# The order of three products in the attention sums: hi by hi, lo by hi, hi by lo

## The reference

```python
xn = layernorm(x)
q, k, v = xn @ wq.T + bq, xn @ wk.T + bk, xn @ wv.T + bv
attn = softmax((q @ k.T) * 256 ** -0.5)
lora = up_aux @ (lora_up @ (lora_down @ down_aux))
out = x + attn @ v + (xn @ W.T + b) + xn @ lora.T
```

## Time and profile before

| what | before |
|---|---|
| median of 3 runs | 518.73 us (518.38 to 518.86) |
| the profiled execution | 518.57 us |
| its span, first to last instruction | 516.8 us |
| granted TensorE clock, mean | 1.000 |
| PE busy | 506.3 us (98%) in 2948 products |
| PEld busy | 448.6 us (87%) in 2948 loads |
| DVE, ACT, POOL busy | 71%, 54%, 72% |

### The profile page before, as it was taken

How to read it: one execution, slowest core, us unless ns; L and a number is a source line. 1 busy time by engine, 2 the same in 40 slices (tenths; PEclk the granted TensorE clock), 3 DMA queues, 4 the chain that set the end, 5 groups by cost and what they waited for, 6 DMA issues and landing times.

```text
span 516.8 us, 8100 instructions
## 1 busy us (share of the span) xinstructions
PE 506.3 (98%) x2948; PEld 448.6 (87%) x2948; DVE 367.4 (71%) x839; ACT 276.6 (54%) x589; POOL 373.7 (72%) x221
## 2 busy tenths in 40 slices
PE   5999999999999999999999999999999999999997
PEld 4677897989989898898989989898998989899897
DVE  4789866867589584885868767696758748376594
ACT  3746667365744747267381655736474462724450
POOL 2834785986789966999669979699678976671730
PEclk9999999999999999999999999999999999999999
DMA  8020004000040003200050100501002010000001
GB/s 238 39 82 0 1 33 173 1 41 2 26 179 1 41 1 109 96 2 41 1 197 8 42 2 0 204 1 42 0 35 90 1 42 1 41 1 2 41 9 74
DMA packets 8694, 25.04 MB, mean 48 GB/s; under 512 B 1850, under 2 KB 3792, under 8 KB 7760
## 3 DMA queue, kind: packets, MB, share of 16 engines
q1 hardware_dynamic: 7328, 24.38, 13.0%
q10 hardware_dynamic: 1328, 0.16, 0.2%
HBM read 16.15 MB, written 8.39 MB: 47 GB/s over the span
## 4 chain that ended last, share of the span: by engine, by line
PE 94%; DVE 1%; ACT 1%; issue 0%; DVEq 0%
PE o_ps L1078 12%; PE o_ps L1080 12%; PE o_ps L1079 12%; PE g_ps L998 10%; PE g_ps L1000 10%; PE g_ps L999 10%; PE s_ps L998 8%; PE s_ps L999 8%; PE s_ps L1000 8%; PE o_ps L998 1%; PE o_ps L999 1%; PE o_ps L1000 1%; ACT prod L607 1%; PE s_ps L1078 0%; PE s_ps L1080 0%
## 5 line engine op out<-in xcount | busy, mean ns | idle before, releaser
L507 POOL TENSOR_TENSOR p_lo<-s,p_hi 128x1024 fp32r<-128x1024 f32 x60 | 144.3, 2439 | 40.0 <-ACT p_hi L657 40.0
L650 ACT ACTIVATE s<-s,e 128x512 f32<-128x512 f32 x128 | 84.3, 714 | 116.3 <-DVE s L848 116.3
L1078 PE MATMUL o_ps<-v_hi,p_hi 128*128 128x258 f32 x480 | 136.5, 284 | 0.0
L1080 PE MATMUL o_ps<-v_hi,p_lo 128*128 128x258 f32 x480 | 136.0, 283 | 0.0
L1079 PE MATMUL o_ps<-v_lo,p_hi 128*128 128x256 f32 x480 | 135.8, 283 | 0.0
L1079 PEld LDWEIGHTS o_ps<-v_lo,p_hi 128*128 128x128 f32 x480 | 91.5, 191 | 1.6
L1078 PEld LDWEIGHTS o_ps<-v_hi,p_hi 128*128 128x128 f32 x480 | 90.2, 188 | 1.6
L1080 PEld LDWEIGHTS o_ps<-v_hi,p_lo 128*128 128x128 f32 x480 | 91.2, 190 | 0.0
L807 DVE SCALAR_TENSOR_TENSOR tile_max<-s_ps,e,tile_max 128x512 f32<-128x512 f32 x80 | 59.9, 748 | 32.9 <-PE s_ps L1000 30.7
L998 PE MATMUL s_ps<-xt_hi,zt_hi 128*128 128x512 f32 x192 | 75.0, 390 | 0.0
L999 PE MATMUL s_ps<-xt_lo,zt_hi 128*128 128x512 f32 x192 | 74.7, 389 | 0.0
(11 more groups left out here) (157 smaller groups left out, 988.8 us busy)
## 6 DMA issues: line engine op xcount, KB each, us to landing
out<-base SPq DMA_DIRECT2D x15, 512.0 KB, 2.7
x_sb<-in_L_attn_x SPq DMA_DIRECT2D x7, 1024.0 KB, 7.8
x_t<-in_x_t SPq DMA_DIRECT2D x6, 1024.0 KB, 5.8
x_sb<-in_L_attn_x SPq DMA_DIRECT2D x4, 256.0 KB, 6.7
out<-base SPq DMA_DIRECT2D x4, 128.0 KB, 1.9
s<-in_L_attn_wk SPq DMA_DIRECT2D x1, 256.0 KB, 3.1
s<-in_L_attn_wq SPq DMA_DIRECT2D x1, 256.0 KB, 6.2
s<-in_L_attn_wv SPq DMA_DIRECT2D x1, 256.0 KB, 6.9
```

The source lines that it names most:

```text
L507: nc.gpsimd.tensor_tensor(p_pair(g, p_lo_sb, j), s_pair(j), p_pair(g, p_hi_sb, j).bitcast(f32), ALU.subtract).then_inc(p_lo_made, 1)
L650: nc.scalar.activation(s[:, n, :], s[:, n, :], ACT.Exp, bias=e[b % 2][:, n:n + 1]).then_inc(p_made, 1)
L1078: nc.tensor.matmul(o[:, 0:D + ONES], hi, v_hi[i][:, n, 0:D + ONES], start=first, stop=False)
L1080: mm = nc.tensor.matmul(o[:, 0:D + ONES], lo, v_hi[i][:, n, 0:D + ONES], start=False, stop=last)
```

## The change

In `add_pair` the second and third product change places. The product of p_hi by v_lo is now the last of a tile and carries the stop flag of the last tile; the product of p_lo by v_hi stands between. `split_products` keeps its order.

```diff
                     nc.tensor.matmul(o[:, 0:D + ONES], hi, v_hi[i][:, n, 0:D + ONES], start=first, stop=False)
-                    nc.tensor.matmul(o[:, 0:D], hi, v_lo[i][:, n, :], start=False, stop=False)
-                    mm = nc.tensor.matmul(o[:, 0:D + ONES], lo, v_hi[i][:, n, 0:D + ONES], start=False, stop=last)
+                    nc.tensor.matmul(o[:, 0:D + ONES], lo, v_hi[i][:, n, 0:D + ONES], start=False, stop=False)
+                    mm = nc.tensor.matmul(o[:, 0:D], hi, v_lo[i][:, n, :], start=False, stop=last)
                 return mm
```

## The result

The kernel after takes 515.78 us (median of 6 runs), the one before 518.73: a ratio of 0.9945 (95% interval 0.9935 to 0.9956), 2.95 us faster, 0.55% by the ratio.

What follows compares the result with a forecast made beforehand. The prediction took PE, never waiting in the sums, to bound the kernel. Its terms, 0 + 0 + 0 + 0 - 0.001 us, left the profiled 518.57 us, so it said 518.6 us, range 517.3 to 519.8.

Steps and rivals of the forecast that it cites:

- Step 1: Products of the sums: columns plus 13.3 ns each, 361.6 ns per tile in either order; change 0.
- the rule of the prediction: Product time as columns at 2.4 GHz plus 13.3 ns: 120.8 ns for 258 columns, 120.0 for 256, 2.89 us a sum.
- Step 2: Weight loads in each tile: p_hi, p_lo, p_hi instead of p_hi, p_hi, p_lo, still three loads; taken as 0.
- The bounds beside it: Limits for the order of weights: gain of 20 ns per twelve products, 2.6 us; loss of 10 ns, 1.3 us.
- The sign that was to tell repeat from partner: Changed interval between product starts: first to second means repeated load; second to third or third to next means a partner.
- Step 3: Moving operands in each tile: v_hi, v_hi, v_lo instead of v_hi, v_lo, v_hi, changing what streams beside a load; taken as 0.
- Steps 4 and 5: PE's waits, including for p_lo: 0; end of a sum, last product two columns shorter: 0.8 ns sooner, cost 0.
- the repeated load: Two p_hi loads in a row cost the longer step; 0.3 to 2.6 us faster, priced 1.3, 517.3 us; chance 0.16.
- Colliding partners: A start slips where a load meets its new moving operand; 1.3 us slower, 519.9 us; chance 0.10.
- the shared weight: Neighbouring p_hi products save the fixed step today, lost after the change; 6.8 us slower, 525.4 us; chance 0.02.

Runs made afterwards that it cites:

- h: Kernel before, its order kept, with 256 columns in every product but the first of a sum (output incomplete): 515.80 us, ratio 0.9945.
- i: Kernel after, its order kept, with 256 columns in every product but the first of a sum (output incomplete): 515.35 us, ratio 0.9932 to before.
- k: Kernel before, its order kept, with four columns of ones instead of two (260 columns in two of three products): 516.84 us, ratio 0.9966.
- d: Kernel before with tile order p_lo by v_hi, p_hi by v_hi, p_hi by v_lo: 515.69 us, ratio 0.9942.
- f: Kernel before with tile order p_lo by v_hi, p_hi by v_lo, p_hi by v_hi: 518.53 us, ratio 0.9997.
- c: Kernel before with tile order p_hi by v_lo, p_hi by v_hi, p_lo by v_hi, except each sum's first tile: 517.40 us, ratio 0.9977.
- e: Kernel before with tile order p_hi by v_lo, p_lo by v_hi, p_hi by v_hi, except each sum's first tile: 516.70 us, ratio 0.9964.

## Why the prediction was wrong, point by point

What bounds the kernel: right. PE had no waits in the sums, and what the products gave up, 2.97 us in the traces, reached the end in full (2.95 by the medians).

Step 1, columns and fixed steps: this failed, and the rest followed from it. The 13.3 ns beyond the columns were read from 512-column products and put on the short ones, and sums of 2.89 then looked like the floor. Measured, a 256-column product costs 118 ns (h, i), 11.3 beyond its columns. By that, an estimate of a sum without excess is 24 x 118 + 16 x 2 / 2.4 = 2845 ns; the sums before stood 0.04 to 0.06 us above it, the sums after, at 2.855, have next to no excess. The estimate isn't a proven floor: for k it gives 24 x 118 + 16 x 4 / 2.4 = 2859 ns, and k took 2.85 us. That the rule of the prediction gave 2.89, the length measured, was a coincidence: the step that was too large stood in for the excess.

Step 2, the order of weights at 0: right in its value, shown by d and f. The bounds beside it were the useful part: 20 ns in every twelve products, 2.6 us. That the sums gave back just these 2.6 us is partly luck, for the bound was read from one sum behind another: its twelve gave back 40 ns by rows rounded to 10 (1.46 to 1.42), the sums behind 512-column products about half of that. The sign that was to tell repeat from partner didn't work: the interval from first to second product shrank most (0.50 to 0.47), which was to mean the repeat, and d shows that it wasn't the repeat. "There is next to no excess that another order could remove" is the statement that was wrong.

Step 3, the order of moving operands at 0: this is the term of the sum that failed. It was weighed only as partner of a load, and it measured -2.6 us in the sums and -0.4 us behind them: d and the kernel after, which share only the order of moving operands, have the same 451.00 us, f and the kernel before the same 453.97. Why this order costs less stays open.

Steps 4 and 5, waits and the end of a sum: right; PE's three waits are still those of the setup.

The rivals: the repeated load named the right sign, and its upper end, 2.6 us, is what the sums gave back, but that is luck: its mechanism is refuted by d. Colliding partners and the shared weight did not come; by the repeated loads of d at full speed, nothing is lost or gained by keeping a weight beside its like.

## What to carry to other kernels

Where TensorE is never waiting, compare starts of short products with a variant of their own length, not with a rule from longer ones: here the excess to be gained stood in the unevenness of the steps (0.11 to 0.13), while the sums looked like the floor. The order of products that share an accumulation can be chosen; none of the six orders costs an instruction, and here they spread over 3 us. Take in what follows the short products, which can eat a part of the gain (c, e). Such a gain hangs on lengths and row spacing (it was gone with rows 320 words apart), so it has to be measured again when either changes.

## What the runs showed of the hardware

- More columns can be faster: 260 columns in two of three products gave sums of 2.85 us where 258 gave 2.89 to 2.91, in the old order.
- The spacing of the moving rows in SBUF changes the length of a sum even where no product repeats the row of the one before: in the old order with 258 columns 2.89 and 2.91 (288 words), 2.88 (320), 2.86 and 2.88 (272), and 2.87 when only v_lo's rows were moved. Buffers that may have moved along are not ruled out.
- The order of a sum's products changes the products behind it: twelve 512-column products took 2.75 us in c and e, 2.72 in the kernel after.
- A weight loaded twice in a row takes as long as a fresh one in the same place (190 ns), and costs nothing.
